# Cross-attention on one core: score products on stacks that come through DRAM, one pass each, and context products in pairs

## The chip, the cores and the metric

One core of a Trainium2 chip runs the whole program. The metric is device time in microseconds. The kernel before was timed three times: 1824.36, 1825.4 and 1828.56 us, median 1825.4.

## The reference

Sixteen sequences of 512 queries `x` and 512 keys `ctx_1024`, width 512, 16 heads of 32, all in fp32:

```
Q = x @ Wq.T + bq;  K = ctx @ Wk.T + bk;  V = ctx @ Wv.T + bv      (split in 16 heads of 32)
scores = Q K^T / sqrt(32), -1e9 where mask == 0
ctx = softmax(scores) V                                            (heads joined again)
y = ctx @ Wo.T + bo + x
out = (y - mean(y)) / sqrt(var(y) + 1e-5) * ln_g + ln_b
```

## The kernel before

**Tiling.** Four heads make a group (`HG`), four groups a sequence, 64 groups in all. A group is worked in four blocks of 128 keys: 256 blocks `y`, 16 to a sequence. Everything repeats with the sequence, so a block is named below by its place 0 to 15 in it (`y % 16`). Every engine runs one loop over `y`, and each holds its instructions in the order written there; semaphores join them. SP issues all DMAs, from one queue.

**Precision.** An operand of a projection or a score is split into a rounded part (`hi`) and the rest (`lo`), and a product is three: hi hi, lo hi, hi lo.

**What a block holds on TensorE** (loop at L885): two scorings. One is a look ahead (`ring`, L768, six blocks early), 128 queries by 512 keys for each of the four heads; VectorE takes the row maxima out of it (`row_max`, L597). The other is the block's own (`exp_banks`, L777), 128 keys by 512 queries; ScalarE has put the mask there first (`seed`, L454) and takes the exponential after it (`exp`, L480). Both come as products of 32 rows, one head each: four of them, two of each scoring, lie side by side in the array, three parts after each other, in two waves. Behind the second wave the maxima are subtracted by four products of two rows (`subtract_maxima`, L786), then the context of the block before is multiplied (`context`, L801, 32 columns a head, four side by side), and every fourth block the sums of the probabilities (`sum_probs`, L821). Blocks 13, 14, 15 and 1 transpose a part of the mask (`turn_mask`, L830). Between all this lies one projection tile, written down in `Plan.SLOT`: kinds K, Q, V (12 products) and O (four fp32 products, the output), its first half at the end of block `y` and its second half in block `y + 1` between the waves (`projection`, L835; lines L874 and L877).

**What follows a tile.** There is one bank for projections. A K or Q tile is rounded out of it by ScalarE (`evacuate`, L500) and its rest is taken by VectorE (`finish_tile`, L624); V needs ScalarE alone, O two additions on VectorE (L614, L618). The first half of the next tile waits for that. VectorE's order in a block is row maxima 0 and 1, `finish_tile`, row maxima 2 and 3, then mask and sums. ScalarE's order is evacuate, exp, seed, exp, seed, then casts, a normalised row or a part of the mask.

**Weights and maxima.** Split K and Q weights wait in DRAM (`w_scratch`) and come back by tile (`load_weights`, L247); a slot of three is taken again when the tile three before is done. The maxima of a group go to DRAM and return as two rows for each head (`move_maxes`, L286), which wave 1 of the group's first block needs.

**GpSimd** adds probabilities up (L372, L380), takes the rests of the inputs (L357) and scales rows.

Of the kernel before, what the change touches and what calls it, by code (L numbers as in the profile page):

```python
# [13 lines left out]
NB = 16  # L14
L = 512
# [19 lines left out]
START = -14  # L35
END = UNITS + 2
LAST = GROUPS - 1
KS, QS, PS, CS, RAW, WS = 4, 3, 4, 6, 8, 3


class Plan:
# [5 lines left out]
    SLOT = {0: ("V", 0, 3), 1: ("K", 0, 3), 2: ("O", -1, 0), 3: ("Q", 0, 3),  # L47
# [3 lines left out]
    CASTS = {2: ((0, 0), (0, 1)), 3: ((0, 2), (0, 3)), 4: ((1, 0), (1, 1)), 5: ((1, 2), (1, 3))}  # L51
    SPLITS = {4: ((0, 0), (0, 1), (0, 2)), 5: ((0, 3), (1, 0), (1, 1)), 6: ((1, 2), (1, 3))}
    MASKS = {13: 0, 14: 1, 15: 2, 1: 3}
    INVERSE, NORMED, SCALED = (3, 4, 3, 3), (4, 7, 7, 7), (6, 8, 8, 10)
# [65 lines left out]
def xattn_program(nc, x, xT, cT, mask, WqT, WkT, WvT, WoT, bq, bk, bv, bo, ln_g, ln_b, out):  # L120
    w_scratch = nc.dram_tensor("w_scratch", (2 * NG, P, 2, NK, P), FP32, kind="Internal").ap()
    max_scratch = nc.dram_tensor("max_scratch", (2, HG, 2, HG, NC, D), FP32, kind="Internal").ap()
    with ExitStack() as ctx:
# [12 lines left out]
        q = sb("q", [P, QS, 2, L], FP32R)  # L136
        k = sb("k", [P, KS, 2, L], FP32R)
        max_rows = sb("max_rows", [P, 2, L], FP32R)
# [3 lines left out]
        minus = sb("minus", [P, P], FP32R)  # L142
# [10 lines left out]
        ident = sb("ident", [P, P])  # L153
# [46 lines left out]
        max_loaded = [sem(f"max_loaded{n}") for n in range(2)]  # L200
# [23 lines left out]
        def _(sp):  # L224
# [52 lines left out]
            for t in range(NK):  # L277
                load_raw(0, 1, t)
# [6 lines left out]

            def move_maxes(g):  # L286
                sp.wait_ge(max_turned, g + 1)
                if g >= 2:
                    sp.wait_ge(max_loaded[g % 2], 2 * FULL * (g // 2))
                    sp.wait_ge(scored, NC * (g - 1))  # L290
# [3 lines left out]
                for part in range(2):  # L294
                    sp.dma_start(
                        max_rows[part::D, g % 2, :].bitcast(FP32).rearrange(
                            "h (c b i) -> h c b i", c=NC, b=HG),
                        max_scratch[g % 2, :, part].rearrange("b h c i -> h c b i")).then_inc(
                            max_loaded[g % 2], FULL)

            for y in range(START, END):
                if PLAN.max_group(y) is not None:
                    move_maxes(PLAN.max_group(y))
                if y == -8:
                    scratch(1, (total[:, :, :], rows[:, :, :]), wq_split, wq_scratch)
                if y == -7:
                    scratch(0, (ctxT[:, 0:NG], probs[:, 3]), wk_split, wk_scratch)
# [7 lines left out]
                seq, at = y // UPS + 1, y % UPS  # L315
                if at == 5 and seq < NB:
                    for t in range(NK):
                        load_raw(seq, 2, t)
                if at == 7 and seq + 1 < NB:
                    for t in range(NK):  # L320
                        load_raw(seq + 1, 0, t)
                if at == 11 and seq + 1 < NB:
                    for t in range(NK):
                        load_raw(seq + 1, 1, t)
# [13 lines left out]
        def _(pool):  # L338
            nc.gpsimd.memset(ident[:, :], 0.0).then_inc(consts_made, 1)
# [4 lines left out]
            nc.gpsimd.memset(minus[:, :].bitcast(FP32), -1.0).then_inc(consts_made, 1)  # L344
            pool.wait_ge(consts_made, 6)
            nc.gpsimd.affine_select(out=ident[:, :], in_=ident[:, :], compare_op=ALU.not_equal,
                                    fill=1.0, base=0, pattern=[[-1, P]],
                                    channel_multiplier=1).then_inc(consts_made, 1)
            pool.wait_ge(consts_made, 7)
            nc.gpsimd.tensor_scalar(ident_bf[:, :], ident[:, :], -1.0, None,  # L350
# [94 lines left out]
        def _(act):  # L445
# [23 lines left out]
            def exp(u, wave):  # L469
                act.wait_ge(scored, u + 1)  # L470
                if u == PS - 1 and wave == 0:
                    act.wait_ge(wk_scratch, 2 * FULL)
                if u >= PS and wave == 0:
                    act.wait_ge(ctx_mm, u - PS + 1)
                    g, kc = divmod(u - PS, NC)
                    if kc == NC - 1:
# [7 lines left out]
            def evacuate(tile):  # L484
# [8 lines left out]
                else:  # L493
                    b_, to, slots = (bq_s, q, QS) if kind == "Q" else (bk_s, k, KS)
                    g = seq * NG + n
                    if g >= slots:
                        act.wait_ge(scored, NC * (g - slots + 1))
                    if g == 0:
                        act.wait_ge(*((bq_scaled, 1) if kind == "Q" else (qk_bias_loaded, 2 * FULL)))
                    nc.scalar.activation(to[:, g % slots, 0], proj_bank[:, 0], ACT.Identity,  # L500
# [9 lines left out]
            def cast(seq, use, t):  # L510
                raw_wait(act, seq, use, t)
                if seq:
                    act.wait_ge(proj_done, PLAN.no["KQ"[use], seq - 1, NG - 1] + 1)
# [3 lines left out]
            act.wait_ge(consts_made, 6)  # L517
            for y in range(START, END):
                tile = PLAN.tile(y - 1)
                if tile and tile[0] != "O":  # L520
                    evacuate(tile)
                for wave in range(2):
                    if 0 <= y < UNITS:
                        exp(y, wave)
                    if 0 <= y + 1 < UNITS:
                        seed(y + 1, wave)
                for c in PLAN.casts(y, PLAN.CASTS):
# [11 lines left out]
        def _(dve):  # L539
# [25 lines left out]
            first_tile(2, wk_raw[:, :, 1])  # L565
# [3 lines left out]
            dve.wait_ge(bq_scaled, 1)  # L569
            dve.wait_ge(wv_loaded, FULL)  # L570
            split(probs[:, 2], wv_hi[:, :, :], wv_lo[:, :, :], wv_split)

            def prologue(y):
                if y == -7:
                    split(wq_raw, by_tile(total[:, :, :]), by_tile(rows[:, :, :]), wq_split)
                if y == -6:
                    split(wk_raw, by_tile(ctxT[:, 0:NG]), by_tile(probs[:, 3]), wk_split)
                    dve.wait_ge(consts_loaded, 4 * FULL)
                    nc.vector.tensor_copy(recipT[:, :, :], bv_s[:, :].unsqueeze(2).to_broadcast(
                        [P, NG, P])).then_inc(bv_wide, 1)  # L580
                if y == -3:
# [27 lines left out]
            def finish_tile(tile):  # L609
# [10 lines left out]
                elif kind != "V":  # L620
                    b_, to, slots = (bq_s, q, QS) if kind == "Q" else (bk_s, k, KS)
                    at = (seq * NG + n) % slots
                    dve.wait_ge(hi_out, PLAN.qk[tile] + 1)
                    nc.vector.scalar_tensor_tensor(  # L624
                        out=to[:, at, 1], in0=proj_bank[:, 0], scalar=b_[:, n:n + 1],
                        in1=to[:, at, 0].bitcast(FP32), op0=ALU.add,
# [52 lines left out]
            for y in range(START, END):  # L679
                prologue(y)  # L680
                row_max(y, 0)
                row_max(y, 1)
                if PLAN.max_group(y) is not None:
                    turn_max(PLAN.max_group(y))
# [44 lines left out]
        def _(pe):  # L729
            pe.wait_ge(consts_made, 8)  # L730
# [16 lines left out]
            def scores(y, wave):  # L747
                item = PLAN.score(y, 2 * wave)
                if item:
                    _, g, c, _ = item  # L750
                    n = PLAN.ring[item]
                    if n >= 1:
                        pe.wait_ge(ring_free, n)
                    if c == 0 and wave == 0:
                        pe.wait_ge(lo_out, PLAN.qk["Q", g // NG, g % NG] + 1)
                if 0 <= y < UNITS:
                    gb, kc = divmod(y, NC)
                    if kc == 0 and wave == 1:
                        pe.wait_ge(max_loaded[gb % 2], 2 * FULL * (gb // 2 + 1))
                    if kc == 0 and wave == 0:  # L760
                        if gb % NG == 0:
                            pe.wait_ge(lo_out, PLAN.qk["Q", gb // NG, gb % NG] + 1)
                    pe.wait_ge(seeded, 2 * y + wave + 1)
                for part, (a, b) in enumerate(((0, 0), (1, 0), (0, 1))):
                    for h in (2 * wave, 2 * wave + 1):
                        if item:
                            rows_h = slice(h * D, (h + 1) * D)
                            mm = nc.tensor.matmul(  # L768
                                ring[:, (n + h % 2) % 2],
                                q[rows_h, g % QS, a, c * P:(c + 1) * P],  # L770
                                k[rows_h, g % KS, b, :], start=part == 0, stop=part == 2)
                    if item and part == 2:
                        mm.then_inc(ring_filled, 2)
                    for h in (2 - 2 * wave, 3 - 2 * wave):
                        if 0 <= y < UNITS:
                            rows_h = slice(h * D, (h + 1) * D)
                            nc.tensor.matmul(  # L777
                                exp_banks[:, h], k[rows_h, gb % KS, b, kc * P:(kc + 1) * P],
# [177 lines left out]
```

## Time and profile before

| | us |
|---|---|
| median of three runs | 1825.4 |
| the profiled execution | 1827.31 |
| its span, first to last instruction | 1825.4 |
| TensorE matmuls busy | 1744.5 |
| ScalarE busy | 1346.8 |
| GpSimd busy | 1287.9 |
| VectorE busy | 1147.2 |

Busy times are unions over the span. A matmul's end is modelled, and matmuls run into each other, so the time of a matmul here is the distance from its start to the start of the next. DMA moved 163.02 MB at a mean 89 GB/s; the one queue of the program took 26.1% of 16 engines' span.

### The profile page before, as it was taken

The page shows a single profiled execution, that of the slowest core. Times are in us where ns is not written, and L with a number is a line of the kernel's source. Part 1 is how long each engine was busy: PE and PEld are TensorE (multiplying, and loading weights), DVE is VectorE, ACT ScalarE, POOL GpSimd, SP SyncE. Part 2 cuts the span into 40 slices and gives each one's busy share as a digit, 9 for nine tenths or more (in the row PEclk, how much of TensorE's full clock was granted, in tenths as well). Part 3 has the DMA queues.
Part 4 walks back from the last instruction along what each step waited for, and adds up shares of the span by engine and source line. Part 5 has one row for each costly group of instructions (what it writes and reads, how often), then busy time and mean ns, then how long its engine had stood idle before and what let it go on. Part 6 is the DMA issues. An engine that isn't in the chain of part 4 may idle for free.

```text
span 1825.4 us, 35936 instructions
## 1 busy us (share of the span) xinstructions
PE 1744.5 (96%) x13556; PEld 870.1 (48%) x13556; DVE 1147.2 (63%) x2836; ACT 1346.8 (74%) x1537; POOL 1287.9 (71%) x836
## 2 busy tenths in 40 slices
PE   5879999999999999999999999999999999999987
PEld 3535455454544545454454545545454454545432
DVE  5646666666666676666667566666666666666643
ACT  2377787777878778787877878777787877778664
POOL 2175686868778687776868767776876868777574
PEclk9989999999999999999999999999999999999978
DMA  8122132222223223222313313232321322321101
GB/s 317 59 94 89 43 117 72 90 105 89 87 78 112 77 88 106 78 83 89 118 60 100 106 59 106 72 110 84 100 97 58 118 71 89 105 66 52 56 8 64
DMA packets 87258, 163.02 MB, mean 89 GB/s; under 512 B 25648, under 2 KB 25648, under 8 KB 87088
## 3 DMA queue, kind: packets, MB, share of 16 engines
q1 hardware_dynamic: 87088, 160.74, 26.1%
q8 instruction: 109, 1.79, 0.4%
q14 instruction: 61, 0.50, 0.1%
HBM read 138.68 MB, written 22.02 MB: 88 GB/s over the span
## 4 chain that ended last, share of the span: by engine, by line
PE 79%; ACT 8%; DVE 7%; issue 5%; DMA 0%; SPq 0%; POOL 0%; DVEq 0%; ACTq 0%; POOLq 0%
PE proj_bank L877 35%; PE ring L768 20%; PE ctx_bank L801 9%; PE proj_bank L874 6%; DVE ring L597 4%; PE ring L821 4%; PE exp_banks L786 3%; ACT probs L480 2%; ACT q L500 2%; ACT exp_banks L454 2%; PE exp_banks L777 1%; ACT k L500 1%; PE ring L830 1%; ACT c_hi L514 1%; PE exp_banks L911 1%
## 5 line engine op out<-in xcount | busy, mean ns | idle before, releaser
L597 DVE CUSTOM_DVE_ANT_0 ring<-ring,bias 128x512 f32<-128x512 f32 x1024 | 687.0, 712 | 382.2 <-PE ring L768 381.8
L480 ACT ACTIVATE probs<-exp_banks 128x1024 f32<-128x1024 f32 x512 | 522.5, 1021 | 223.4 <-PE exp_banks L786 223.4
L454 ACT CAST exp_banks<-biasT 128x1024 f32<-128x1024 bf16 x512 | 520.6, 1017 | 23.7 <-ACT probs L480 0.7
L768 PE MATMUL ring<-k,q 32*128 32x512 f32 x3072 | 498.3, 428 | 16.7 <-DVE maxes L597 10.2
L777 PE MATMUL exp_banks<-q,k 32*128 32x512 f32 x3072 | 501.4, 430 | 3.5 <-ACT exp_banks L454 3.5
L768 PEld LDWEIGHTS ring<-k,q 32*128 32x128 f32 x3072 | 249.6, 184 | 281.4 <-DVE maxes L597 140.0
L372 POOL TENSOR_TENSOR total<-total,probs 128x2048 f32<-128x2048 f32 x63 | 289.0, 4588 | 89.5 <-ACT probs L480 87.4
L372 POOL TENSOR_TENSOR total<-probs 128x2048 f32<-128x2048 f32 x63 | 289.4, 4593 | 52.4 <-ACT probs L480 52.4
L380 POOL TENSOR_TENSOR total<-total,probs 128x1024 f32<-128x1024 f32 x126 | 298.9, 2394 | 9.0
L801 PE MATMUL ctx_bank<-probs,v 128*32 128x512 f32 x2048 | 281.2, 622 | 0.6 <-DVE ctxT L656 0.6
L777 PEld LDWEIGHTS exp_banks<-q,k 32*128 32x128 f32 x3072 | 251.4, 186 | 16.4 <-ACT exp_banks L454 11.5
L877 PE MATMUL proj_bank<-c_hi,w_tile 128*128 128x512 f32 x512 | 168.4, 410 | 15.6 <-POOL c_lo L357 15.0
L387 POOL CAST max_parts<-maxes 128x16 fp32r<-128x16 f32 x64 | 12.6, 196 | 239.0 <-DVE maxes L597 239.0
L877 PE MATMUL proj_bank<-x_hi,w_tile 128*128 128x512 f32 x512 | 167.7, 409 | 5.9 <-DVE k L624 5.9
L597 DVE DVE_READ_ACCUMULATOR2_ANT maxes<- 128x1 f32 x1024 | 143.9, 141 | 0.0
L877 PEld LDWEIGHTS proj_bank<-c_hi,w_tile 128*128 128x128 f32 x512 | 92.8, 191 | 69.8 <-issue 41.8
L877 PEld LDWEIGHTS proj_bank<-x_hi,w_tile 128*128 128x128 f32 x512 | 92.4, 190 | 60.8 <-DVE k L624 19.4
L877 PE MATMUL proj_bank<-wo,ctxT 128*128 128x512 f32 x240 | 119.0, 618 | 0.0
L874 PE MATMUL proj_bank<-wo,ctxT 128*32 128x512 f32 x960 | 114.4, 592 | 0.0
L786 PE MATMUL exp_banks<-max_rows,minus 2*128 2x512 f32 x1024 | 110.2, 397 | 0.0
L877 PE MATMUL proj_bank<-c_lo,w_tile 128*128 128x512 f32 x256 | 109.0, 426 | 0.0
L877 PE MATMUL proj_bank<-x_lo,w_tile 128*128 128x512 f32 x256 | 108.8, 425 | 0.0
(81 smaller groups left out, 2095.4 us busy)
## 6 DMA issues: line engine op xcount, KB each, us to landing
w_tile<-w_scratch SPq DMA_DIRECT2D x125, 512.0 KB, 4.0
raw<-cT_dram SPq DMA_DIRECT2D x64, 256.0 KB, 4.8
raw<-xT_dram SPq DMA_DIRECT2D x64, 256.0 KB, 4.2
raw<-mask_dram SPq DMA_DIRECT2D x64, 256.0 KB, 2.8
rows<-x_dram SPq DMA_DIRECT2D x64, 256.0 KB, 3.2
out_dram<-rows SPq DMA_DIRECT2D x64, 256.0 KB, 2.0
max_rows<-max_scratch SPq DMA_DIRECT2D x128, 8.0 KB
probs<-WkT_dram SPq DMA_DIRECT2D x1, 1024.0 KB, 5.5
```

What stands on the lines that cost most here:

```text
L372: nc.gpsimd.tensor_tensor(total[:, :, :], first, probs[:, u % PS], ALU.add).then_inc(adds, 1)
L380: nc.gpsimd.tensor_tensor(total[:, heads], total[:, heads], probs[:, u % PS, heads], ALU.add).then_inc(adds, 1)
L454: nc.scalar.copy(exp_banks[:, 2 - 2 * wave:4 - 2 * wave, :], biasT[:, kc:kc + 1, :].to_broadcast([P, 2, L])).then_inc(seeded, 1)
L480: nc.scalar.activation(probs[:, u % PS, 2 - 2 * wave:4 - 2 * wave, :], exp_banks[:, 2 - 2 * wave:4 - 2 * wave, :], ACT.Exp).then_inc(exps, 1)
L597: nc.vector.tensor_tensor_reduce(out=ring[:, n % 2], in0=ring[:, n % 2], in1=bias[:, c], scale=1.0, scalar=LOWEST, op0=ALU.subtract, op1=A ...
L768: mm = nc.tensor.matmul(ring[:, (n + h % 2) % 2], q[rows_h, g % QS, a, c * P:(c + 1) * P], k[rows_h, g % KS, b, :], start=part == 0, stop= ...
L777: nc.tensor.matmul(exp_banks[:, h], k[rows_h, gb % KS, b, kc * P:(kc + 1) * P], q[rows_h, gb % QS, a, :], start=False, stop=False, skip_gr ...
L786: mm = nc.tensor.matmul(exp_banks[:, h], minus[two, :], max_rows[two, g % 2, :], start=False, stop=True, skip_group_check=True)
L801: mm = nc.tensor.matmul(ctx_bank[h * D:(h + 1) * D, 0], v[:, m % 5, col:col + D], probs[:, u % PS, h], start=kc == 0, stop=kc == NC - 1)
L821: mm = nc.tensor.matmul(ring[h * D:(h + 1) * D, n % 2], ones[:, :], total[:, h], start=True, stop=True)
L874: nc.tensor.matmul(proj_bank[d:d + D, 0], a[:, d:d + D], b, start=m == 0, stop=False)
L877: mm = nc.tensor.matmul(proj_bank[:, 0], a, b, start=m == 0, stop=m == len(parts) - 1)
```

## The change

- **Stacks.** `q` and `k` go. A K or Q tile is rounded into one buffer `qk_hi` and its rest into one buffer `qk_lo`; SP stores both in DRAM (`keep_halves`, two DMAs of 256 KB), and six DMAs of 256 KB for each group (`stack`) bring them back so that each head has hi, lo, hi of Q over hi, hi, lo of K in partitions 0 to 95. A stack is loaded eight blocks ahead of its group and used from six blocks ahead. The next K or Q tile can be rounded when both stores of the last have landed.
- **Scores.** A head's product is now one of 96 rows. The block's own scoring has 98: the maxima lie in rows 96 and 97 of the Q stack, against a -1 in the K stack, and `subtract_maxima` goes. `scored` counts waves, so an exponential waits for its own two heads. The maxima are needed before wave 0.
- **Context.** Even blocks hold the context products of the two blocks before; odd blocks hold none. An O tile's first half is no longer cut in columns of 32.
- **Order.** ScalarE evacuates after the first exp and seed. VectorE turns the maxima at the start of a block. Tiles have other places, and so have casts, rests, and loads. Buffers shrink: probs 4 to 3, contexts 6 to 5, raw inputs 8 to 7, weight slots 3 to 2 (a load waits for the tile two before).

```
-KS, QS, PS, CS, RAW, WS = 4, 3, 4, 6, 8, 3
+SS, PS, CS, RAW, WS = 3, 3, 5, 7, 2
-    SLOT = {0: ("V", 0, 3), 1: ("K", 0, 3), 2: ("O", -1, 0), 3: ("Q", 0, 3),
-            4: ("O", -1, 1), 5: ("O", -1, 2), 6: ("O", -1, 3), 7: ("K", 1, 0),
-            8: ("Q", 1, 0), 9: ("V", 1, 0), 10: ("K", 1, 1), 11: ("Q", 1, 1),
-            12: ("K", 1, 2), 13: ("V", 1, 1), 14: ("V", 1, 2), 15: ("Q", 1, 2)}
+    SLOT = {0: ("V", 0, 3), 1: ("Q", 0, 3), 2: ("O", -1, 0), 3: ("O", -1, 1),
+            4: ("O", -1, 2), 5: ("K", 1, 0), 6: ("Q", 1, 0), 7: ("O", -1, 3),
+            8: ("K", 1, 1), 9: ("Q", 1, 1), 10: ("V", 1, 0), 11: ("K", 1, 2),
+            12: ("Q", 1, 2), 13: ("K", 1, 3), 14: ("V", 1, 1), 15: ("V", 1, 2)}
+    def stack_group(self, y):
+        g, k = divmod(y + 8, NC)
+        return g if k == 0 and 0 <= g < GROUPS else None
...
+            def keep_halves(tile):
...
+                sp.wait_ge(hi_out, i + 1)
+                sp.dma_start(kept[0], qk_hi[:, :].bitcast(FP32)).then_inc(halves_kept, FULL)
+                sp.wait_ge(lo_out, i + 1)
+                sp.dma_start(kept[1], qk_lo[:, :].bitcast(FP32)).then_inc(halves_kept, FULL)
+            def stack(kind, g):
+                if g >= SS:
+                    sp.wait_ge(scored, 2 * NC * (g - SS + 1))
...
+                sp.wait_ge(halves_kept, 2 * FULL * (PLAN.qk[kind, g // NG, g % NG] + 1))
...
+                for part, src in enumerate((0, 1, 0) if kind == "Q" else (0, 0, 1)):
+                    sp.dma_start(
+                        dst[part * D:(part + 1) * D, g % SS * HG:(g % SS + 1) * HG, :].bitcast(FP32),
+                        kept[src].rearrange("(h d) n -> d h n", d=D)).then_inc(done[g % SS], FULL)
...
             for y in range(START, END):
+                if PLAN.stack_group(y) is not None:
+                    stack("K", PLAN.stack_group(y))
+                    stack("Q", PLAN.stack_group(y))
                 if PLAN.max_group(y) is not None:
                     move_maxes(PLAN.max_group(y))
...
+                tile = PLAN.tile(y - 1)
+                if tile and tile[0] in "QK":
+                    keep_halves(tile)
...
                 for ahead, kinds in ((2, "QK"), (4, "O")):
...
                 if at == 11 and seq + 1 < NB:
-                    for t in range(NK):
+                    for t in range(3):
                         load_raw(seq + 1, 1, t)
...
                 else:
+                    i = PLAN.qk[tile]
+                    if i:
+                        act.wait_ge(halves_kept, 2 * FULL * i)
...
+            def score(y, h):
...
+                if n >= 2:
+                    pe.wait_ge(ring_free, n - 1)
...
+                nc.tensor.matmul(ring[:, n % 2], q_stack[0:3 * D, at, c * P:(c + 1) * P],
+                                 k_stack[0:3 * D, at, :], start=True,
+                                 stop=True).then_inc(ring_filled, 1)
+            def shifted_scores(u, wave):
...
+                pe.wait_ge(seeded, 2 * u + wave + 1)
+                for h in (2 - 2 * wave, 3 - 2 * wave):
+                    at = g % SS * HG + h
+                    mm = nc.tensor.matmul(exp_banks[:, h],
+                                          k_stack[0:3 * D + 2, at, kc * P:(kc + 1) * P],
+                                          q_stack[0:3 * D + 2, at, :], start=False, stop=True,
+                                          skip_group_check=True)
+                mm.then_inc(scored, 1)
...
             for y in range(START, END):
                 prologue(y)
-                scores(y, 0)
+                shifted_scores(y, 0)
+                score(y, 0)
+                score(y, 1)
                 if PLAN.tile(y - 1):
                     projection(PLAN.tile(y - 1), 1)
-                scores(y, 1)
-                if 0 <= y < UNITS:
-                    subtract_maxima(y)
-                if 0 <= y - 1 < UNITS:
-                    context(y - 1)
+                shifted_scores(y, 1)
+                score(y, 2)
+                score(y, 3)
+                for u in (y - 2, y - 1):
+                    if y % 2 == 0 and 0 <= u < UNITS:
+                        context(u)
```

## Rows read from the trace of the kernel before

**Rows 1.** The page: busy time of each engine, share of the span, instructions.
```profile
PE 1744.5 (96%) x13556; PEld 870.1 (48%) x13556; DVE 1147.2 (63%) x2836; ACT 1346.8 (74%) x1537; POOL 1287.9 (71%) x836
```

**Rows 2.** Timeline of SP (start us, us): the maxima's store, one sequence apart.
```profile
927.95 0.32 SPq L291 DMA_DIRECT2D max_scratch<-max_turns  x1
...
1035.94 0.32 SPq L291 DMA_DIRECT2D max_scratch<-max_turns  x1
```

**Rows 3.** Timeline of PE: end of block 11, a K or Q tile around it.
```profile
907.52 0.40 PE L877 MATMUL proj_bank<-c_lo,w_tile 128*128 128x512 f32 x1
907.85 0.50 PE L768 MATMUL ring<-k,q 32*128 32x512 f32 x2
...
908.64 0.41 PE L786 MATMUL exp_banks<-max_rows,minus 2*128 2x512 f32 x4
908.99 1.06 PE L801 MATMUL ctx_bank<-probs,v 128*32 128x512 f32 x8
909.98 0.73 PE L877 MATMUL proj_bank<-x_hi,w_tile 128*128 128x512 f32 x2
...
911.34 0.50 PE L768 MATMUL ring<-k,q 32*128 32x512 f32 x2
```

**Rows 4.** Timeline of PE: context and an O tile's two halves.
```profile
955.98 1.07 PE L801 MATMUL ctx_bank<-probs,v 128*32 128x512 f32 x8
956.86 1.90 PE L874 MATMUL proj_bank<-wo,ctxT 128*32 128x512 f32 x16
958.69 0.50 PE L768 MATMUL ring<-k,q 32*128 32x512 f32 x2
...
959.59 1.98 PE L877 MATMUL proj_bank<-wo,ctxT 128*128 128x512 f32 x4
961.50 0.50 PE L768 MATMUL ring<-k,q 32*128 32x512 f32 x2
```

**Rows 5.** Timeline of PE: a part of the mask and what follows it.
```profile
930.29 0.40 PE L830 MATMUL ring<-ident_bf,bias 128*128 128x128 bf16 x4
930.49 0.47 PE L877 MATMUL proj_bank<-wv_hi,c_hi 128*128 128x512 f32 x1
```

**Rows 6.** Groups by line: busy us, mean ns of one, idle before, releaser.
```profile
L597 DVE CUSTOM_DVE_ANT_0 ring<-ring,bias 128x512 f32<-128x512 f32 x1024 | 687.0, 712 | 382.2 <-PE ring L768 381.8
L480 ACT ACTIVATE probs<-exp_banks 128x1024 f32<-128x1024 f32 x512 | 522.5, 1021 | 223.4 <-PE exp_banks L786 223.4
L454 ACT CAST exp_banks<-biasT 128x1024 f32<-128x1024 bf16 x512 | 520.6, 1017 | 23.7 <-ACT probs L480 0.7
```

**Rows 7.** Timeline of PE in the start-up, where no context follows a tile.
```profile
45.18 0.40 PE L877 MATMUL proj_bank<-c_lo,w_tile 128*128 128x512 f32 x1
...
47.14 0.73 PE L877 MATMUL proj_bank<-x_hi,w_tile 128*128 128x512 f32 x2 [0.67 <-DVE k L624]
...
63.21 0.40 PE L877 MATMUL proj_bank<-wv_lo,c_hi 128*128 128x512 f32 x1
...
65.46 0.38 PE L830 MATMUL ring<-ident_bf,bias 128*128 128x128 bf16 x4 [0.95 <-DVE maxes L597]
```

**Rows 8.** Timeline of SP: issue of one weight tile and four raw loads.
```profile
984.62 0.40 SPq L255 DMA_DIRECT2D w_tile<-w_scratch  x1
985.06 1.85 SPq L238 DMA_DIRECT2D raw<-cT_dram  x4
```

**Rows 9.** Two stretches: engines' busy us, then PEclk, DMA share, GB/s.
```profile
986.00:991.00 5.00, 5.00 (x44) 2.04 (x40) 3.30 (x7) 3.12 (x4) 4.86 (x2) 1.00 1.00 342
988.50:989.00 0.50, 0.50 (x6) 0.04 (x4) 0.06 (x2) 0.00 (x0) 0.36 (x2) 1.00 0.91 201
```

**Rows 10.** The page's DMA issues: KB each, median us from issue to landing.
```profile
out_dram<-rows SPq DMA_DIRECT2D x64, 256.0 KB, 2.0
```

**Rows 11.** PE after its longest idle time, and the stretch behind it, as Rows 9.
```profile
25.36 1.22 PE L877 MATMUL proj_bank<-x_hi,w_tile 128*128 128x512 f32 x2 [5.27 <-DVE k L624]
...
25.40:29.70 4.30, 4.30 (x10) 3.47 (x11) 3.33 (x2) 0.22 (x1) 0.00 (x0) 0.50 0.19 70
```

More of the change, by code:

```diff
@@ L199, in xattn_program @@
         max_stored = sem("max_stored")
-        max_loaded = [sem(f"max_loaded{n}") for n in range(2)]
+        max_loaded = [sem(f"max_loaded{n}") for n in range(SS)]
+        halves_kept, minus_ones = sem("halves_kept"), sem("minus_ones")
+        q_stacked = [sem(f"q_stacked{n}") for n in range(SS)]
+        k_stacked = [sem(f"k_stacked{n}") for n in range(SS)]
         tail_done, tail_biased = sem("tail_done"), sem("tail_biased")
@@ L276, in _ @@
             load_weight(WqT, probs[:, 1], wq_loaded)
-            for t in range(NK):
+            for t in range(NK - 1):
                 load_raw(0, 1, t)
@@ L315, in _ @@
                 seq, at = y // UPS + 1, y % UPS
+                if at == 3 and 0 < seq < NB:
+                    load_raw(seq, 1, 3)
                 if at == 5 and seq < NB:
[L317 removed]
+                    for t in range(3):
                         load_raw(seq, 2, t)
[L319 to L321 removed]
+                if at == 6:
+                    if seq < NB:
+                        load_raw(seq, 2, 3)
+                    if seq + 1 < NB:
+                        for t in range(3):
+                            load_raw(seq + 1, 0, t)
+                if at == 8 and seq + 1 < NB:
+                    load_raw(seq + 1, 0, 3)
                 if at == 11 and seq + 1 < NB:
[L323 removed]
+                    for t in range(3):
                         load_raw(seq + 1, 1, t)
@@ L469, in exp @@
             def exp(u, wave):
-                act.wait_ge(scored, u + 1)
-                if u == PS - 1 and wave == 0:
-                    act.wait_ge(wk_scratch, 2 * FULL)
+                act.wait_ge(scored, 2 * u + wave + 1)
                 if u >= PS and wave == 0:
-                    act.wait_ge(ctx_mm, u - PS + 1)
                     g, kc = divmod(u - PS, NC)
-                    if kc == NC - 1:
+                    act.wait_ge(ctx_mm, u - PS + (2 if g == LAST else 1))
+                    if g == LAST:
+                        pass
+                    elif kc == NC - 1:
                         act.wait_ge(adds, 4 * g + 4)
@@ L526, in _ @@
                         seed(y + 1, wave)
+                    tile = PLAN.tile(y - 1)
+                    if wave == 0 and tile and tile[0] != "O":
+                        evacuate(tile)
                 for c in PLAN.casts(y, PLAN.CASTS):
@@ L620, in finish_tile @@
                 elif kind != "V":
-                    b_, to, slots = (bq_s, q, QS) if kind == "Q" else (bk_s, k, KS)
-                    at = (seq * NG + n) % slots
                     dve.wait_ge(hi_out, PLAN.qk[tile] + 1)
                     nc.vector.scalar_tensor_tensor(
-                        out=to[:, at, 1], in0=proj_bank[:, 0], scalar=b_[:, n:n + 1],
-                        in1=to[:, at, 0].bitcast(FP32), op0=ALU.add,
+                        out=qk_lo[:, :], in0=proj_bank[:, 0],
+                        scalar=(bq_s if kind == "Q" else bk_s)[:, n:n + 1],
+                        in1=qk_hi[:, :].bitcast(FP32), op0=ALU.add,
                         op1=ALU.subtract).then_inc(lo_out, 1)
@@ L745, in prologue @@
                     mm.then_inc(bv_wo, 1)
[L747 to L755, printed above, removed]
-                if 0 <= y < UNITS:
[L757 to L778, printed above, removed]
-                                q[rows_h, gb % QS, a, :], start=False, stop=False,
-                                skip_group_check=True)
@@ L782, in subtract_maxima @@
-            def subtract_maxima(y):
-                g = y // NC
-                for h in range(HG):
-                    two = slice(h * D, h * D + 2)
-                    mm = nc.tensor.matmul(
-                        exp_banks[:, h], minus[two, :], max_rows[two, g % 2, :],
-                        start=False, stop=True, skip_group_check=True)
+            def score(y, h):
+                item = PLAN.score(y, h)
+                if not item:
+                    return
+                _, g, c, _ = item
+                n = PLAN.ring[item]
+                if n >= 2:
+                    pe.wait_ge(ring_free, n - 1)
+                if c == 0 and h == 0:
+                    pe.wait_ge(q_stacked[g % SS], STACKED * (g // SS + 1))
+                    pe.wait_ge(k_stacked[g % SS], STACKED * (g // SS + 1))
+                at = g % SS * HG + h
+                nc.tensor.matmul(ring[:, n % 2], q_stack[0:3 * D, at, c * P:(c + 1) * P],
+                                 k_stack[0:3 * D, at, :], start=True,
+                                 stop=True).then_inc(ring_filled, 1)
@@ L871, in projection @@
                     a, b = parts[m]
-                    if kind == "O" and half == 0:
-                        for d in range(0, P, D):
-                            nc.tensor.matmul(proj_bank[d:d + D, 0], a[:, d:d + D], b, start=m == 0,
-                                             stop=False)
-                        continue
                     mm = nc.tensor.matmul(proj_bank[:, 0], a, b, start=m == 0,
```

114 lines of the change are left out of this document (66 added, 48 removed).

## The prediction, made before the change was built

> **What bounds the kernel now.** I read the page first: TensorE is busy 96% of the span, the next engine 74% [rows 1]. Then SP's timeline: the same store comes 108.0 us apart [rows 2], so the span is 16 sequences of 108.0 = 1728 and some 97 of start and end. Then TensorE's timeline, start to start. A slot of 512 columns takes 0.23: between 907.85 and 908.64 lie three slots, 0.79 [rows 3]. The first is 0.34, and so is the last before another way of cutting the array (907.52 to 907.85, 908.64 to 908.99): a switch between products of 32 rows, 32 columns and the full array costs some 0.21, half before and half behind it. A block has five. Context takes 0.99 before a switch [rows 3] and 0.88 before work cut the same way [rows 4]. A block with a K, Q or V tile is 3 slots, 7, 4, context, 5, with switches: 0.90 + 1.83 + 1.13 + 0.99 + 1.36 = 6.21. An O block is 6.65 (halves of 1.83 and 1.91 [rows 4]), sums add 1.26 (0.88, a switch's worth, a short wait), a mask part 0.20 [rows 5]. 12 x 6.21 + 4 x 6.65 + 4 x 1.26 + 4 x 0.20 = 107. TensorE sets the time in all blocks.
>
> **TensorE's own work after.** Scoring is 8 full slots, 1.84, where there were 7 slots in two switched stretches, 2.03. Slots of fewer rows than the array part (the two-row maxima behind 32-row products) cost no switch [rows 3], so I count none between 96, 98 and 128 rows. What is left is one excursion to context in two blocks: 0.10 + 0.88 + 1.00 + 0.11 = 2.09 for both contexts. So an odd block with a K, Q or V tile is 20 slots, 4.6, an even one 6.7; sums add 0.87, an O half is 1.71 (1.91 less a switch [rows 4]) in place of 1.61 or 1.15, a mask part 0.30, since the slot behind it is longer. Blocks 0 to 15: 7.6, 4.9, 7.25, 5.25, 8.2, 4.7, 6.7, 5.15, 7.7, 4.6, 6.7, 4.6, 7.6, 4.9, 7.0, 4.9: 97.9. Alone that saves 10 a sequence.
>
> **What comes late once context is gone from odd blocks.** Between a tile's end and the next tile's start there stood 0.90 to 1.13 of scores and 0.99 of context. In an odd block there are four slots. The start-up shows the chain without context: 45.18, last product of a tile, to 47.14, first of the next, with ScalarE and VectorE between: 1.96 [rows 7]. In an odd block that gives a start 4.26 into the block where the slots end at 3.45: a stall of 0.81 for K or Q (blocks 7, 9), about the same for O's two additions (3, 5), 0.11 more each for a weight load that is no longer covered; V needs ScalarE alone and just fits. A mask part also needs row maximum 2 out of its bank. Behind a V tile: scored at 3.4, VectorE 0.71 [rows 6], and 0.2 as in the start-up row that waited 0.95 [rows 7]: 4.34, a stall of 0.89 (blocks 1, 15). In block 13 VectorE takes a Q tile's rest first, and the mask part starts at 5.0: 1.56. Sum: 4 x 0.92 + 2 x 0.89 + 1.56 = 7.0. So 97.9 + 7.0 = 104.9, or 3.1 less than 108.0.
>
> ScalarE has 4.1 of exp and seed a block [rows 6] and some 84 of work a sequence [rows 1]; it falls up to 0.8 behind in blocks 9 and 11 and the even block after takes that in. Exps that start after their own wave help it. GpSimd adds the same sums; with three probability buffers the first add must end before the exponential two blocks later, which it does by 1.9. I cost both at nothing; uncovered they cost that lateness, up to 0.8. Turning the maxima before the row maxima delays VectorE by half a microsecond where it has more. Stores and stacks in blocks 0, 4 and 8 end several microseconds before their readers.
>
> **The place where the queue fills.** SP is one queue. In its iteration 11 it loads the weights of tile 13, and with two slots that waits for tile 11's last product, in block 12 at 2.7. Behind it stand, in this order: weights (512 KB), three raw loads (768 KB), six stack loads (1536 KB), then the two stores of tile 11 (512 KB). ScalarE may not round tile 12 before those stores land, and it wants to in block 13 at 2.77, that is at 7.6 + 2.77 = 10.35 from block 12's start. Issue alone: 0.4 to 0.46 each [rows 8], twelve of them, 5.4, so the last store is issued at 8.1; at 2.0 to landing [rows 10] it would land at 10.1, just in time if data cost nothing. Data: first bytes some 1.1 behind the issue, at 3.8; at 342 GB/s [rows 9] 256 KB take 0.77, so weights, raw loads and stores, seven such pieces, 5.3. A stack load writes 32 partitions only, which no row shows. Bounds: 0.74 (a little over the mean of the same stretch; with all engines at share 1.00 it can't be faster) and 1.3 (201 GB/s, the slowest half microsecond in it [rows 9]). I take 1.0, between them, for want of a row near either end. 3.8 + 5.3 + 6 x 1.0 + 0.6 for the last packets = 15.7: late by 5.3 (3.8 to 7.1). Nothing hides it: VectorE stands behind ScalarE in `finish_tile`, row maximum 2 behind that, the mask part behind that, and TensorE behind the mask. It is all added to block 13, in 15 of the sequences.
>
> TensorE is then idle for some 6.5 in one go. The one idle time of that size before, 5.27, was followed by a granted clock of 0.50 (1.2 of 2.4 GHz) for 4.3 of full work [rows 11], a loss of 2.1. I take 2.0 (0 to 2.2). 104.9 + 5.3 + 2.0 = 112.2, or 4.2 more than 108.0.
>
> **The rest.** Start: one tile more (K 3), its weights by way of DRAM one tile earlier, two more DMA trips: +6 (0 to +12). End: the last blocks have no projections; waves that go on by themselves and fewer switches: -6 (-12 to 0). Sum: 1825.4 + 15 x 4.2 = 1888 as a span, 1890 as the profiled execution's own time (it was 1827.31), 1888 for the median, which stands 1.9 below that execution. Own range with the bounds (3.8 + 0 to 7.1 + 2.2, and the ends): 1840 to 1930.
>
> **A rule that makes it worse.** The widest SP traffic here runs at 342 GB/s into 128 partitions [rows 9]. The Trainium skill, SBUF — State Buffer on-chip working memory, section Door 1: The DMA port swizzle, says that 32 neighbouring partitions reach half of the DMA ports, so such a load runs at about half rate. No row of before has such a load. By it a stack load would be near 1.2 by the page's asymptote, an estimate, and the lateness near 6.4.
>
> **Rivals.**
> - Stack loads at little more than half the rate, 1.3 each, the slowest stretch of a full queue [rows 9], because each reaches a quarter of the partitions, and six stand in a row before the stores. Late by 3.8 + 5.3 + 7.8 + 0.6 - 10.35 = 7.1, clock 2.2: 104.9 + 9.3 = 114.2, +93, 1918. Against it: no row shows that it is the partitions that matter. The rule above is this case. 0.15.
> - Faster: the queue does not hold block 13, because the stores land within 10.35. For it the data would have to move at some 570 GB/s (3.4 MB in the 6.0 between 3.8 and 9.8), or the stores be issued before the stacks by a path that I don't see. Then only the odd stalls stay, 104.9: 16 x -3.1 = -50, 1776. For it speaks that most of its sum rests on TensorE rows that repeat to 0.02, while the queue's order is read from the text alone. It ends where lateness and clock reach 3.1. 0.30.
> - Nothing to see: fast stacks, late by 3, the clock stays: 104.9 + 3.0, 1825. 0.05.
> - The stacks don't do what they say: 96 or 98 rows count as another cut of the array, and each scoring stretch keeps its two switches: 97.9 + 4 x 0.21 x 16 = 111.3, with stalls about 116, +130: 1950. The two-row products speak against it [rows 3]. 0.02.
>
> **How the numbers follow.** The forecast has 0.48, the others as given. Slower by over 0.2% (about what a measurement of this kernel can tell from no change) is 0.48 + 0.15 + 0.02 = 0.65, faster 0.30, within 0.05. The range has to hold part of the faster case: 1770 to 1920 leaves out 0.1 on either side.
>
> **What would show it.** Right: the SP store that begins each sequence's round comes about 112 apart; scores stand between projections at 0.23 a slot without a longer first or last; a context pair takes 1.9; in blocks 3, 5, 7 and 9 TensorE idles 0.8 before the next tile's first half; once a sequence ScalarE waits 4 to 7 for a store of `qk_hi` or `qk_lo`, VectorE's `qk_lo` behind it, and TensorE's mask part behind that, with the granted clock at 0.50 after it. Wrong: a period near 105 and no such wait, or slots with 0.34 at both ends of each scoring.

## The result, and the profile after

The changed kernel takes 1917.12 us (median of four runs, 1913.55 to 1921.29), the kernel before 1826.98 beside it: a ratio of 1.0495, 95% interval 1.0465 to 1.0526. It is slower by 5%, on the side of the forecast (1888) and inside its range (1770 to 1920), close to the upper end. It comes out where the rival with slow stack loads stood (1918); how far that is luck is said below.

The page after, in parts (span; busy us of the engines; queue; the chain that ended last by line; groups as in [rows 6]; DMA issues as in [rows 10]):

```profile
span 1919.5 us, 24771 instructions
PE 1665.8 (87%) x7716; PEld 1017.4 (53%) x7716; DVE 1154.3 (60%) x2835; ACT 1340.6 (70%) x1537; POOL 1282.7 (67%) x835
...
q1 hardware_dynamic: 180928, 329.08, 59.4%
...
PE proj_bank L913 39%; PE ctx_bank L842 11%; PE exp_banks L826 10%; PE ring L811 9%; DMA stack_scratch<-qk_lo 8%; PE ring L862 2%; SPq L317 2%; ACT qk_hi L550 2%; DVE ring L650 2%; DVE qk_lo L675 1%; PE ring L871 1%; DVE proj_bank L667 1%; DVE rows L671 1%; SPq L247 1%; PE exp_banks L950 1%
...
L826 PE MATMUL exp_banks<-q_stack,k_stack 98*128 98x512 f32 x1024 | 378.1, 452 | 7.3 <-ACT exp_banks L504 7.3
...
L550 ACT ACTIVATE qk_hi<-proj_bank,bq_s 128x512 fp32r<-128x512 f32 x64 | 43.9, 686 | 146.0 <-DMA stack_scratch<-qk_lo 119.5
...
w_tile<-w_scratch SPq DMA_DIRECT2D x126, 512.0 KB, 4.1
k_stack<-stack_scratch SPq DMA_DIRECT2D x192, 256.0 KB, 5.3
q_stack<-stack_scratch SPq DMA_DIRECT2D x192, 256.0 KB, 7.2
stack_scratch<-qk_hi SPq DMA_DIRECT2D x128, 256.0 KB, 2.1
```

TensorE is busy 79 less than before [rows 1] in a span that is 94 longer. The gain in its work is there, as less busy time; what grew is its waiting, and part of what is busy runs at a lower clock. The chain names a DMA that the kernel before did not have: the store of `qk_lo`, 8% of the span. ScalarE's rounding of Q tiles waits 119.5 for it in all.

The store of the maxima, one sequence apart, as in [rows 2] (timeline of SP):

```profile
1222.43 0.32 SPq L327 DMA_DIRECT2D max_scratch<-max_turns  x1
...
1335.05 0.32 SPq L327 DMA_DIRECT2D max_scratch<-max_turns  x1
```

112.6 here; 113.8 in the mean of the 13 sequences from block 0 at 211.1 to block 0 at 1690.7, against 108.0. Blocks 12 and 13 of one sequence on SP (start us, us):

```profile
1317.10 0.32 SPq L264 DMA_DIRECT2D w_tile<-w_scratch  x1
1317.47 1.38 SPq L247 DMA_DIRECT2D raw<-xT_dram  x3
1318.96 1.49 SPq L317 DMA_DIRECT2D k_stack<-stack_scratch  x3
1320.56 1.48 SPq L317 DMA_DIRECT2D q_stack<-stack_scratch  x3
1322.13 0.62 SPq L304 DMA_DIRECT2D stack_scratch<-qk_hi  x1
1322.80 0.45 SPq L306 DMA_DIRECT2D stack_scratch<-qk_lo  x1
1332.07 0.32 SPq L304 DMA_DIRECT2D stack_scratch<-qk_hi  x1
```

The same stretch on ScalarE, VectorE and TensorE (three timelines, in brackets the idle time before and who ended it):

```profile
1331.32 0.69 ACT L550 ACTIVATE qk_hi<-proj_bank,bq_s 128x512 fp32r<-128x512 f32 x1 [6.38 <-DMA stack_scratch<-qk_lo]
```
```profile
1332.04 0.75 DVE L675 SCALAR_TENSOR_TENSOR qk_lo<-proj_bank,bq_s,qk_hi 128x512 fp32r<-128x512 f32 x1 [7.19 <-ACT qk_hi L550]
1332.70 0.69 DVE L650 CUSTOM_DVE_ANT_0 ring<-ring,bias 128x512 f32<-128x512 f32 x1
```
```profile
1324.51 0.39 PE L913 MATMUL proj_bank<-x_lo,w_tile 128*128 128x512 f32 x1
1324.74 0.63 PE L826 MATMUL exp_banks<-q_stack,k_stack 98*128 98x512 f32 x2
1325.20 0.63 PE L811 MATMUL ring<-k_stack,q_stack 96*128 96x512 f32 x2
1333.60 0.58 PE L871 MATMUL ring<-ident_bf,bias 128*128 128x128 bf16 x4 [7.76 <-DVE maxes L650]
```

These rows show one chain, in the order forecast: a store issued at 1322.80 lets ScalarE go at 1331.32, then `qk_lo`, then row maximum 2, then the mask part. Two stretches of it (columns as in [rows 9]):

```profile
1323.50:1328.50 5.00, 2.33 (x11) 1.56 (x9) 1.34 (x5) 1.41 (x2) 0.65 (x1) 1.00 1.07 227
...
1333.60:1336.70 3.10, 3.10 (x11) 2.52 (x12) 1.31 (x4) 1.11 (x2) 2.45 (x3) 0.50 0.50 179
```

While the stacks load, the DMA engines are busy all the time (a share of 1.07) and move 227 GB/s, where [rows 9] had 342 at 1.00. After the wait TensorE works at half its clock (0.50).

### The profile page after: what moved, and what is told of

It reads as the page before. It is cut to its first block, busy times and chain, and to the rows that moved or that the text cites. A ratio compares the mean times of both kernels' runs of the same rounds, so it can differ in the third digit from the quotient of the medians.

```text
span 1919.5 us, 24771 instructions
## 1 busy us (share of the span) xinstructions
PE 1665.8 (87%) x7716; PEld 1017.4 (53%) x7716; DVE 1154.3 (60%) x2835; ACT 1340.6 (70%) x1537; POOL 1282.7 (67%) x835
## 4 chain that ended last, share of the span: by engine, by line
PE 74%; DMA 9%; DVE 7%; SPq 4%; issue 3%; ACT 2%; POOL 1%; DVEq 0%; POOLq 0%; ACTq 0%
PE proj_bank L913 39%; PE ctx_bank L842 11%; PE exp_banks L826 10%; PE ring L811 9%; DMA stack_scratch<-qk_lo 8%; PE ring L862 2%; SPq L317 2%; ACT qk_hi L550 2%; DVE ring L650 2%; DVE qk_lo L675 1%; PE ring L871 1%; DVE proj_bank L667 1%; DVE rows L671 1%; SPq L247 1%; PE exp_banks L950 1%
## 5 line engine op out<-in xcount | busy, mean ns | idle before, releaser
L826 PE MATMUL exp_banks<-q_stack,k_stack 98*128 98x512 f32 x1024 | 378.1, 452 | 7.3 <-ACT exp_banks L504 7.3
L811 PE MATMUL ring<-k_stack,q_stack 96*128 96x512 f32 x1024 | 335.0, 406 | 14.1 <-DVE maxes L650 11.0
L842 PE MATMUL ctx_bank<-probs,v 128*32 128x512 f32 x2048 | 255.6, 617 | 0.0
L826 PEld LDWEIGHTS exp_banks<-q_stack,k_stack 98*128 98x128 f32 x1024 | 197.7, 194 | 108.4 <-issue 68.9
L913 PE MATMUL proj_bank<-wo,ctxT 128*128 128x512 f32 x480 | 231.7, 605 | 17.6 <-DVE qk_lo L675 8.8
L811 PEld LDWEIGHTS ring<-k_stack,q_stack 96*128 96x128 f32 x1024 | 198.1, 194 | 72.9 <-DVE maxes L650 23.3
L675 DVE SCALAR_TENSOR_TENSOR qk_lo<-proj_bank,bq_s,qk_hi 128x512 fp32r<-128x512 f32 x64 | 48.1, 751 | 191.6 <-ACT qk_hi L550 191.6
L871 PE MATMUL ring<-ident_bf,bias 128*128 128x128 bf16 x256 | 28.0, 239 | 155.4 <-DVE maxes L650 155.4
L913 PEld LDWEIGHTS proj_bank<-wo,ctxT 128*128 128x128 f32 x480 | 85.9, 189 | 118.2 <-issue 82.8
L550 ACT ACTIVATE qk_hi<-proj_bank,bq_s 128x512 fp32r<-128x512 f32 x64 | 43.9, 686 | 146.0 <-DMA stack_scratch<-qk_lo 119.5
```

The lines of the kernel that those rows point to most:

```text
L550: nc.scalar.activation(qk_hi[:, :], proj_bank[:, 0], ACT.Identity, bias=b_[:, n:n + 1]).then_inc(hi_out, 1)
L675: nc.vector.scalar_tensor_tensor(out=qk_lo[:, :], in0=proj_bank[:, 0], scalar=(bq_s if kind == "Q" else bk_s)[:, n:n + 1], in1=qk_hi[:, :] ...
L811: nc.tensor.matmul(ring[:, n % 2], q_stack[0:3 * D, at, c * P:(c + 1) * P], k_stack[0:3 * D, at, :], start=True, stop=True).then_inc(ring_ ...
L826: mm = nc.tensor.matmul(exp_banks[:, h], k_stack[0:3 * D + 2, at, kc * P:(kc + 1) * P], q_stack[0:3 * D + 2, at, :], start=False, stop=Tru ...
L842: mm = nc.tensor.matmul(ctx_bank[h * D:(h + 1) * D, 0], v[:, m % 5, col:col + D], probs[:, u % PS, h], start=kc == 0, stop=kc == NC - 1)
L871: mm = nc.tensor.matmul(ring[:, n % 2, c * P:(c + 1) * P], bias[:, c, kc * P:(kc + 1) * P], ident_bf[:, :], start=True, stop=True)
```

## The experiments

**1. The queue's order alone.** Block 12 issues stacks, stores, then weights and raw loads:

```
+                if y % UPS == 12 and PLAN.tile(y + 1):
+                    load_weights(PLAN.tile(y + 1))
...
-                    if tile and tile[0] in kinds:
+                    if tile and tile[0] in kinds and not (y % UPS == 11 and kinds == "QK"):
...
-                if at == 11 and seq + 1 < NB:
+                if at == 12 and seq + 1 < NB:
```

> Changed kernel, SP's order only: the weights of tile 13 and the three raw x loads go from iteration 11 to iteration 12, behind the stacks and the two stores of tile 11. Queue theory (the stores of tile 11 stand behind 3.4 MB and hold block 13): the stores land some 8 after block 12's start, ScalarE's wait for them goes, block 13 falls from about 14.8 to 6.4 and block 14 to 7.0 with no clock loss, a sequence from 113.2 to about 105.2, the whole from 1917 to about 1795. Rival (the wait is only where some other shortage, say of the DMA engines at 59% of the span, comes out): the lateness moves to another block and the time stays within 20 of 1917.

1780.96 (ratio 0.9744 to before, 0.9728 to 0.9761): 136 less than the changed kernel, from one move of four loads. SP and TensorE in the same place of a sequence:

```profile
1319.51 1.27 SPq L317 DMA_DIRECT2D k_stack<-stack_scratch  x3
1320.88 1.32 SPq L317 DMA_DIRECT2D q_stack<-stack_scratch  x3
1325.01 0.34 SPq L304 DMA_DIRECT2D stack_scratch<-qk_hi  x1
1325.75 0.34 SPq L306 DMA_DIRECT2D stack_scratch<-qk_lo  x1
1326.18 0.40 SPq L264 DMA_DIRECT2D w_tile<-w_scratch  x1
```
```profile
1331.33 0.63 PE L828 MATMUL exp_banks<-q_stack,k_stack 98*128 98x512 f32 x2
1331.80 0.63 PE L813 MATMUL ring<-k_stack,q_stack 96*128 96x512 f32 x2
1333.81 0.38 PE L873 MATMUL ring<-ident_bf,bias 128*128 128x128 bf16 x4 [1.39 <-DVE maxes L652]
```

Block 13 takes 6.45 to 6.48 and block 14 6.86 to 6.88 in every sequence, a sequence 104.76, and ScalarE never waits for a store. The bytes are the same, so the DMA engines are not short overall: the rival falls. The queue's order is the cause. The edit takes two things from in front of the stores, the wait for tile 11's last product and 1.28 MB of loads; no run parts them. The whole came out 14 under the 1795 expected: a sequence falls by 9.0, not 8, and block 0 starts 5.8 earlier, which was not expected.

**2. Only the stores moved.** In block 12 `keep_halves` stands before `stack`; weights and raw loads stay ahead of both.

> Changed kernel with one move: in iteration 12 the two stores of tile 11 go ahead of the six stack loads; weights and raw loads stay ahead of both. Queue theory: the stores land at about 10 from block 12's start, so ScalarE waits 0 to 1; the stacks are issued 3 later and their data now ends about 18 from block 12's start, while block 14's first score wants them at 14.8, so some 3 of lateness comes out in block 14. Block 13 near 7, block 14 near 10; about 5 a sequence less, 1840. Rival (it is the stores' own landing that is slow, whatever stands before them): block 13 stays above 12.

1845.89 (1.0108, 1.0092 to 1.0124), where 1840 was expected. Blocks 13 and 14 take about 7.2 and 10.8. ScalarE's wait for the store, then TensorE:

```profile
1385.96 0.69 ACT L553 ACTIVATE qk_hi<-proj_bank,bq_s 128x512 fp32r<-128x512 f32 x1 [0.37 <-DMA stack_scratch<-qk_lo]
```
```profile
1388.24 0.38 PE L874 MATMUL ring<-ident_bf,bias 128*128 128x128 bf16 x4 [1.76 <-DVE maxes L653]
1392.82 1.19 PE L814 MATMUL ring<-k_stack,q_stack 96*128 96x512 f32 x2 [1.69 <-issue]
```

The wait changes its place, as the queue theory had it: the mask part is nearly on time (an idle time of 1.76 before it, 1.39 in experiment 1) and block 14's first score is late. That score waits for a stack: the profile names the load of `q_stack` in two of the 13 sequences in the middle and nothing ("issue") in the other 11. The store's own landing is not slow. Block 14 takes 4.0 more than in experiment 1. About 1.8 of it is this idle time; the rest is slower products, at a mean granted clock of 0.65 from 1388 to 1392 and 0.62 from 1392.8 to 1397.

**3. The same bytes into all partitions.** Each load of a stack goes to 128 partitions of one head's place:

```
-                        dst[part * D:(part + 1) * D, g % SS * HG:(g % SS + 1) * HG, :].bitcast(FP32),
-                        kept[src].rearrange("(h d) n -> d h n", d=D)).then_inc(done[g % SS], FULL)
+                    sp.dma_start(dst[:, g % SS * HG + part, :].bitcast(FP32),
+                                 kept[src]).then_inc(done[g % SS], FULL)
...
-                    nc.vector.memset(k_stack[3 * D:3 * D + 2, :, :].bitcast(FP32),
+                    nc.vector.memset(k_stack[3 * D:3 * D + 2, 3:4, :].bitcast(FP32),
...
```

The scores take their operands from the three places filled, the block's own with 96 rows, and the memset in the start covers a twelfth of its columns.

> Changed kernel with each of the six stack loads of 256 KB written to all 128 partitions of one head's place in place of 32 partitions of four; same bytes, same count, same order. The scores and their maxima are then not the reference's, and the block's own scoring has 96 rows. Partitions theory (a load into 32 partitions runs at 200 to 250 GB/s): with 128 partitions the six loads take 4.6 in place of about 8, block 13 falls by about 3.5 to 11.3, the whole to about 1860, and the rate in the burst is near 342 GB/s. Rival (what is slow is reading back what was just stored, or the turn between stores and loads): block 13 stays at 14.8 and the time at 1917.

1871.16 (1.0247, 1.0228 to 1.0266), where 1860 was expected. Block 13 takes 12.0 in the mean (11.3 expected). ScalarE's wait, and a stretch that ends before the stores' bytes begin, by a count of the bytes from the first load on:

```profile
1403.72 0.69 ACT L549 ACTIVATE qk_hi<-proj_bank,bq_s 128x512 fp32r<-128x512 f32 x1 [4.70 <-DMA stack_scratch<-qk_lo]
```
```profile
1396.50:1400.50 4.00, 3.41 (x15) 2.44 (x13) 2.38 (x6) 2.04 (x2) 1.65 (x2) 1.00 0.99 350
```

350 GB/s against 227, at DMA engines about as busy (0.99 and 1.07) and with the same number of packets in the whole run: a load into 32 partitions is what was slow, not reading back what was stored. At 227 a load of 256 KB takes 1.15, at 350 0.75; six make 2.4 of the 2.7 by which a sequence is shorter than in the changed kernel. The Trainium skill, SBUF — State Buffer, section Door 1: The DMA port swizzle, gives half the ports to 32 neighbouring partitions and 189 against 328 GB/s as measured for 1 MiB, a ratio of 0.58. By that rule and these rows the trace agrees, at a ratio of 0.65.

**4. Context in every block again, on top of 1.**

```
-                for u in (y - 2, y - 1):
-                    if y % 2 == 0 and 0 <= u < UNITS:
+                for u in (y - 1,):
+                    if 0 <= u < UNITS:
```

> As the reordered kernel, and context of one block in every block again (each in the block after its own) in place of two in every even block. Cover theory (odd blocks stall because nothing stands between a tile's end and the next tile's start): pairs of blocks with K, Q or O in the odd one go from 5.5 + 6.7 to 5.8 + 5.8, the idle times of 0.6 to 0.7 go, two switches more a pair cost 0.33; blocks 1, 13 and 15 lose 0.5 each. 3 to 4 a sequence less than the reordered kernel, about 1740. Rival (the pair is worth its switches and the stalls are small): 3 a sequence more, about 1840.

1751.77 (0.9595, 0.9581 to 0.961), 29 less than experiment 1. Odd blocks on TensorE, with context ahead of block 1's mask part and of block 3's first half of an O tile:

```profile
1128.98 0.63 PE L813 MATMUL ring<-k_stack,q_stack 96*128 96x512 f32 x2
1129.54 1.06 PE L844 MATMUL ctx_bank<-probs,v 128*32 128x512 f32 x8
1130.54 0.40 PE L873 MATMUL ring<-ident_bf,bias 128*128 128x128 bf16 x4
...
1142.05 1.06 PE L844 MATMUL ctx_bank<-probs,v 128*32 128x512 f32 x8
1143.05 1.98 PE L915 MATMUL proj_bank<-wo,ctxT 128*128 128x512 f32 x4
```

A sequence takes 102.85, and no idle time of TensorE over 0.4 is left in its middle. The sign was as forecast, the size half of it (1.9 a sequence, not 3 to 4). Blocks 10 and 11, which lose no idle time, take 0.33 more together (11.32 to 11.65), as counted. Blocks 2 and 3, and 6 and 7, gain 0.50 and 0.56, nearly the 0.6 expected. What failed are blocks 4 and 5, and 8 and 9: they were to gain as much and lose 0.03 and 0.16, where idle times of 0.35 come up ahead of the sums in blocks 4 and 8. So the pairs of context products cost time in this kernel: two switches saved in two blocks are worth 0.33, and the cover that leaves the odd block is worth more.

**5 and 6. The start.** On top of 4, the memset of the K stack's rows of -1 moved from block -4 to -7; then also the split and the store of the Q weights moved ahead.

```
-                if y == -4:
+                if y == -7:
                     dve.wait_ge(wk_scratch, 2 * FULL)
                     nc.vector.memset(k_stack[3 * D:3 * D + 2, :, :].bitcast(FP32),
...
-                if y == -8:
+                if y == -9:
                     dve.wait_ge(consts_made, 7)
```

> As e4 (reordered, context in every block), and the memset of the K stack's two rows of -1 (one VectorE instruction of 5.18 for 6144 columns of two partitions, in block -4 in the way of a row maximum that TensorE waits for) moved to block -7, where VectorE idles while a weight load is under way. Start theory (part of the start's 31 is this instruction on VectorE's queue): TensorE's idle time of 4.8 at 70 goes, block 0 starts at about 91 in place of 95.6, the whole 1747. Rival (the next stack or store is late at the same place): unchanged within 1.

> As e5, and the split of the Q weights one block earlier on VectorE (block -9, before tile Q 0's rest) and their store in DRAM ahead of tile Q 0's stores on SP. Start theory (the second K or Q pair waits for weights that make the trip through DRAM one after the other, TensorE idle 9 at 38): the weights of Q 1 are back at about 41 in place of 47, block 0 starts at about 85, the whole near 1741. Rival (DMA is full there, so what goes ahead holds something else, K 1's weights): less than 2 is gained.

1747.41 (0.957, 0.9552 to 0.9588) and 1747.01 (0.9571, 0.9549 to 0.9594). Against experiment 4 both are 4 to 5 less, at the edge of what these runs tell apart; the two can't be told from each other. They are the fastest versions here, 4.3% under the kernel before. The memset in experiment 4, then TensorE there, in 5 and in 6:

```profile
69.19 5.18 DVE L634 MEMSET k_stack<- 2x6144 f32 x1 [1.34 <-issue]
```
```profile
75.12 1.46 PE L813 MATMUL ring<-k_stack,q_stack 96*128 96x512 f32 x2 [4.78 <-DVE maxes L652]
```
```profile
74.45 0.73 PE L915 MATMUL proj_bank<-x_hi,w_tile 128*128 128x512 f32 x2 [1.10 <-DVE qk_lo L677]
```
```profile
46.33 1.20 PE L915 MATMUL proj_bank<-x_hi,w_tile 128*128 128x512 f32 x2 [8.20 <-DMA w_tile<-w_scratch]
```

The idle time of 4.8 goes, but block 0 starts only 1.5 earlier (94.1 against 95.6, where 91 was expected), and in the profiled executions 1.1 of that is lost again in the first sequence. So the whole of experiment 5 came out at the 1747 expected, but not by the way expected. In 6 block 0 starts 1.6 earlier again (92.5, where 85 was expected): the wait for Q 1's weights shrinks only from 9.1 in experiment 4 to 8.2, and the gain over 5 is under the 2 that the rival allowed.

**7. ScalarE's order of before, on top of 4** (evacuate ahead of both exponentials).

> As e4, with ScalarE's order of before: it evacuates a tile at the head of a block, ahead of both exponentials. Theory (a tile's end is what matters and ScalarE reaches it on time either way, but now the first exp waits 2 for it and ScalarE's slack goes): the same time within 5 of 1752, ScalarE's idle time before the exponentials gone over to the evacuation. Rival (the later exponentials run into the seeds that TensorE needs): 0.5 to 1 a block in blocks with casts or masks, some 60 more.

1757.69 (0.9621, 0.9607 to 0.9635), 6 more than experiment 4, just over the 5 allowed. In the profiled executions it is 4.6 ahead of block 0 (which starts at 100.1) and 2.2 in the first sequence; a sequence in the middle takes the same 102.8. Once the rest runs, that part of the change makes no difference.

## Why the prediction came out as it did

**TensorE's own work and the odd blocks: right.** The forecast blocks add up to 97.75, which the text has as 97.9. With that, 97.9 of work and 7.0 of stalls made 104.9; experiment 1 has 104.76. Block 13 was put at 6.5 (measured 6.48), 14 at 7.0 (6.87), 1 at 5.8 (5.77). Blocks 2, 5, 7 and 8 are off by 0.3 to 0.4 each, two of them up and two down, and it is luck that this cancels. The two ends' switch costs and the absence of one between 96, 98 and 128 rows hold: in the rows above a product of 128 rows, two of 98 and two of 96 start 0.23 and 0.46 apart. The stalls were sized about right. The idle times in brackets read 0.58 and 0.58 before O's first half in blocks 3 and 5 of experiment 1, 0.63 and 0.47 in 7 and 9, 0.71 before the mask part in 1 and 15, and 1.39 in 13. But a bracket begins at the modelled end of the product before, some 0.40 behind its start, and the forecast counts a slot of 0.23. From start to start the mask parts are late by 0.88 (forecast 0.89) and 1.56 (1.56), and the first halves, with the 0.11 for the weight load, by 0.75 to 0.91 (0.92).

**The full queue: right in mechanism and place, too small.** The step had the last store landing 15.7 after block 12's start, with 1.0 for a stack load between bounds of 0.74 and 1.3. The load takes 1.15 in the rows, and ScalarE could go 16.9 after block 12's start (1331.32 against 1314.4). Six loads at 0.15 more each are 0.9 of these 1.2; the other seven pieces account for most of the rest. The start of the data and its tail, put at 1.1 and 0.6 with no row shown for them, hold in the changed kernel: the first bytes move 0.9 after the issue at 1317.10, and the last some 0.6 ahead of 1331.32. The lower bound of 0.74 rested on the argument that engines at a share of 1.00 can't be faster; experiment 3 moved 400 GB/s at 1.04 from 1400 to 1402, where the stores are, so the argument does not hold, though a stack load into 128 partitions still takes 0.75. ScalarE's waits for such a store are 123.7 in 17 cases; two of them, 4.2 and 14.8, are in the start, and the other 15, one a sequence, have a mean of 7.0, where 5.3 was forecast. At 1.2 a load the forecast's own sum gives about 6.5 (it says 6.4). The rival with slow loads had 7.1, and so the right size of this wait.

**The clock: right.** TensorE idles some 8.5 in one go and is then granted 0.50 (1.2 of 2.4 GHz) in the stretch shown, as [rows 11] had it behind 5.27. From experiment 1 to the changed kernel a sequence grows by 9.1 (113.81 less 104.76); the idle time at the mask part grows by about 7.1 (8.5 against 1.4), so some 1.9 is left for the clock, where 2.0 was forecast. It is worked out from the difference; no run kept the wait without the lower clock.

**The ends: wrong.** I had +6 and -6. Block 0 starts at 104.80 where it started at 73.14, and the last sequence's first block leaves 117.2 to the end where it left 131.2: +31.7 and -14.0. With 15 sequences of +5.1 on the mean that is the 94 of the two spans. The mean is under the +5.8 of the middle because the first sequence, which has no O tiles, takes only 106.3. What the step missed at the start is that stacks, stores and weights all make DRAM trips one after the other there, and that TensorE then idles again and again and works at the low clock. The two trips more were in the forecast, at 6 for everything. TensorE's timeline in the changed kernel, and below it a stretch of the same (columns as in [rows 9]):

```profile
48.09 0.77 PE L913 MATMUL proj_bank<-x_hi,w_tile 128*128 128x512 f32 x1 [10.68 <-DMA w_tile<-w_scratch]
...
77.76 1.47 PE L811 MATMUL ring<-k_stack,q_stack 96*128 96x512 f32 x2 [4.76 <-DVE maxes L650]
90.84 0.58 PE L871 MATMUL ring<-ident_bf,bias 128*128 128x128 bf16 x4 [5.46 <-DVE maxes L650]
```
```profile
40.00:64.00 24.00, 12.98 (x27) 8.77 (x28) 3.55 (x10) 2.01 (x4) 0.00 (x0) 0.51 0.75 222
```

In the kernel before the same 24 us had a granted clock of 1.00 and 21.23 of matmuls. Of the 31.7 the runs settle 5.8 (the queue's order: 99.0 in experiment 1), 3.5 (context, 95.6 in 4) and some 3 (experiments 5 and 6). Experiment 3 has block 0 at 97.2, 7.6 earlier than the changed kernel, by faster stack loads and the shorter memset together; what the loads alone give there was not measured. The rest, above all the wait of 10.68 for the second Q tile's weights, stays open. In the kernel before, the third weight slot held the second K tile's weights from the beginning, which spared one trip; no run tried a third slot beside the stacks.

**The sum.** The span is 94 longer and not 63: 13.5 too little in the middle (15 x 5.1 against 15 x 4.2), 25.7 too little at the start, and 8 at the end the other way, 31 together. The 13.5 hide two errors: the wait and the clock together took 25 more than forecast (134 in 15 sequences where 7.3 each make 110), while the other blocks gave 11 back, most of it in the short first sequence. So the terms of the queue and of the start were off by about the same, 25 and 26, and the end and the other blocks took back 8 and 11: the forecast of 1888 is 29 under the median. The rival's 1918 is nearly exact by luck: it had the wait and the clock right, but nothing for the start (+31.7) or the end (-14.0), and 6.2 a sequence where the mean is 5.1.

## What to carry to other kernels

Where one engine issues all transfers, a lookahead load that waits for compute holds everything queued behind it, and the small store that somebody needs next pays for all bytes ahead of it (8.5 from issue to use at 1322.80, where the median landing of such a store is 2.4): write down, for each wait on that queue, what stands behind it and who needs the last of it. Moving four loads by one iteration was worth 136 here; the reordered kernel as a whole stands 46 under the kernel before. And a bound for a transfer should come from one with the same spread over partitions. Last, a start of 100 us with several trips through DRAM needs its own chain of waits worked out, as the middle had; here it was off by as much as the middle.

## What the runs showed of the hardware

- Loads of 256 KB into 32 partitions moved at 227 GB/s (changed kernel) with the DMA engines about as busy (1.07) as at 350 GB/s into 128 (0.99, experiment 3). The busy share does not show that the loads are slow.
- A VectorE memset of two partitions by 6144 fp32 columns took 5.18, and one by 512 columns 0.48 (experiments 4 and 3).
- One product of 128 rows, two of 98 and two of 96 follow each other at 0.23 each (1324.51 to 1325.20 in the changed kernel), with no switch. Going to column tiles and back costs some 0.21: there, from two products at 1306.04 context starts at 1306.60 (0.10 over two slots), and the product behind it takes 0.34 to the next (1308.45 to 1308.79).
